# A new order of instructions on five engines of a decoder layer: the first group's scores behind the feed-forward tiles

## The reference

```
x = layernorm(x + attention(x))          # 16 heads of 32, LoRA added to the q, k, v, o projections
x = layernorm(x + x * scan(ctx * ctx))   # r = decay * r + ctx*ctx along the sequence
h = gelu(silu(bitlinear(x, w1)))         # 2048 wide; bitlinear: rms norm, round to 8 bits,
h = layernorm(h, ln_g, ln_b)             # weights rounded to -1, 0, 1
x = layernorm(x + bitlinear(h, w2))
```

## Time and profile before

| | |
|---|---|
| median of 3 runs | 1128.77 us (1127.43 to 1133.42) |
| profiled execution | 1124.67 us, its span 1122.9 us |
| busy, share of the span | PE 85%, DVE 79%, ACT 74%, POOL 54% |
| one batch (from `y(j,0)` to `y(j+1,0)`) | 60.9 us |
| mean granted clock of TensorE | 0.945 of full |

### The profile page before, as it was taken

How to read it: one execution, slowest core, us unless ns; L and a number is a source line. 1 busy time by engine, 2 the same in 40 slices (tenths; PEclk the granted TensorE clock), 3 DMA queues, 4 the chain that set the end, 5 groups by cost and what they waited for, 6 DMA issues and landing times.

```text
span 1122.9 us, 23509 instructions
## 1 busy us (share of the span) xinstructions
PE 952.4 (85%) x9388; PEld 653.1 (58%) x9388; DVE 887.3 (79%) x1470; ACT 828.3 (74%) x955; POOL 601.0 (54%) x769
## 2 busy tenths in 40 slices
PE   4878878998989898999999898989899998873424
PEld 2666656675757666665757575766667575531201
DVE  5378858888897979798988989797979898885442
ACT  3456677887879787878788787978787878775651
POOL 3213428384756657482938475565738293747250
PEclk8989898999999999999999999999999999977756
DMA  8512100213131212213221313122221222121112
GB/s 309 208 71 101 43 27 20 69 49 78 49 78 20 75 52 51 62 53 69 48 79 49 78 48 78 20 70 57 50 58 57 69 48 60 49 59 28 40 28 66
DMA packets 106350, 73.67 MB, mean 66 GB/s; under 512 B 91385, under 2 KB 91385, under 8 KB 104450
## 3 DMA queue, kind: packets, MB, share of 16 engines
q1 hardware_dynamic: 105522, 70.34, 23.4%
q10 hardware_dynamic: 720, 1.84, 0.5%
HBM read 41.73 MB, written 8.40 MB: 45 GB/s over the span
## 4 chain that ended last, share of the span: by engine, by line
PE 49%; DVE 31%; ACT 7%; issue 6%; DMA 4%; POOL 2%; SPq 1%; POOLq 0%; ACTq 0%; DVEq 0%
PE bank L1081 17%; PE bank L1202 10%; PE bank L1195 9%; DVE neg_max L793 3%; PE wave L1128 3%; DVE fz L912 3%; DVE h L907 3%; DVE stats L842 3%; PE bank L1140 2%; PE wave L1104 2%; DMA xqT<-xq 2%; PE bank L1144 2%; PE bank L1196 2%; DVE xq L898 2%; DVE rows L858 2%
## 5 line engine op out<-in xcount | busy, mean ns | idle before, releaser
L793 DVE TENSOR_REDUCE neg_max<-wave 128x8 f32<-128x2048 f32 x64 | 146.2, 2285 | 56.8 <-PE wave L1104 56.8
L1195 PE MATMUL bank<-w,xqT 128*128 128x512 fp8e4 x512 | 133.9, 385 | 44.9 <-DMA xqT<-xq 36.9
L479 POOL TENSOR_TENSOR h<-h,g_tile 128x2048 f32<-128x2048 f32 x32 | 148.4, 4638 | 40.4 <-ACT h L642 40.4
L1202 PE MATMUL bank<-w,hqT 128*128 128x512 fp8e4 x512 | 124.7, 400 | 43.3 <-DMA hqT<-h 43.3
L559 ACT ACTIVATE probs<-wave 128x1024 f32<-128x1024 f32 x128 | 124.0, 1021 | 30.9 <-PE wave L1128 30.8
L621 ACT ACTIVATE h<-bank,qx 128x512 f32<-128x512 f32 x128 | 87.0, 687 | 44.6 <-PE bank L1196 44.3
L597 ACT ACTIVATE rows<-rows,rstd 128x512 f32<-128x512 f32 x96 | 74.4, 807 | 55.7 <-POOL rstd L394 19.7
L1202 PEld LDWEIGHTS bank<-w,hqT 128*128 128x128 bf16 x512 | 49.7, 102 | 112.2 <-issue 62.0
L1195 PEld LDWEIGHTS bank<-w,xqT 128*128 128x128 bf16 x512 | 48.5, 99 | 110.6 <-issue 47.1
L378 POOL TENSOR_SCALAR attn_hi<-attn 128x256 fp32r<-128x256 f32 x64 | 26.2, 409 | 157.5 <-DVE attn L826 148.7
L907 DVE TENSOR_TENSOR h<-h,b_tile 128x2048 f32<-128x2048 f32 x32 | 75.5, 2359 | 36.5 <-POOL h L479 36.5
(11 more groups left out here) (151 smaller groups left out, 2821.3 us busy)
## 6 DMA issues: line engine op xcount, KB each, us to landing
ctx_sb<-ctxT SPq DMA_DIRECT2D x16, 512.0 KB, 3.7
rows<-x SPq DMA_DIRECT2D x16, 512.0 KB, 4.0
out<-rows SPq DMA_DIRECT2D x32, 256.0 KB, 2.0
xT_in<-xT SPq DMA_DIRECT2D x15, 512.0 KB, 4.7
h<-w1T SPq DMA_DIRECT2D x4, 1024.0 KB, 5.4
h<-w2T SPq DMA_DIRECT2D x4, 1024.0 KB, 5.6
h<-Wq SPq DMA_DIRECT2D x1, 1024.0 KB, 5.8
h<-Wk SPq DMA_DIRECT2D x1, 1024.0 KB, 9.6
```

The lines of the kernel that those rows point to most:

```text
L479: po.tensor_tensor(h_of(b, q)[:, :], h_of(b, q)[:, :], g_tile[:, :], ALU.mult).then_inc(S["g_mul"], 1)
L793: dv.tensor_reduce(neg_max[:, :, :], wave[:, :, :].rearrange("p j (t k) -> p j t k", t=NT), axis=AX_X, op=ALU.max, negate=True).then_inc(S ...
L1195: pe.matmul(p[:, :], xqT[:, q, kc, :], w1[:, kc, n * FW:(n + 1) * FW], start=(kc == 0), stop=False)
L1202: last = pe.matmul(p[:, :], hqT[:, k, :], w2[:, k, :], start=(k == 0), stop=(k == FC - 1))
```

## The change

The lists of four engines are put in another order, SyncE's list stays.

TensorE: `scores(j,0)` moves from the end of body j-1 to the start of body j, `shiftT(j,0)` between the two halves of `o(j-1,0)`, `shifted(j,0)` behind them. The eight feed-forward tiles so run without anything between them. `weighted(j,3)` stands ahead of `qk(j+1,1)`, and `v(j+1,0)` is split in two around `shiftT(j,3)`. Tiles f take banks 6, 7 and 4 in turn instead of 6 and 7. Since bank 4 is that of `weighted`, f2 waits for `attn_norm(j,3)`, and `weighted(j,0)` for the SiLU of the seventh tile (index 6).

VectorE: `maxima(j,0)` opens the body; `z_max(j-2,0)` stands behind `layernorm2_sum`, `qk_lo(j+1,0)` ahead of `attn_norm(j,2)`, `z_add(j-2,1)` behind `quantise_z(j-2,0)`, `scan(j)` ahead of `qk_lo(j+1,1)` and `quantise_z(j-2,1)`.

ScalarE: `z_square` of both halves stands behind `normalise(2)`, the second one as late as behind `zq_store(j-2,0)`; `probs_of(j,3)` comes ahead of `xq_store(j-1)`, and that ahead of `v_store(j+1,1)`, `normalise(3,j-3,1)` and `ctx_square(j)`; `qk_hi(j+1,1)` stands between the two `silu`.

GpSimd: `inverse_std2` and `x_rms` come ahead of `g_mul(j-2,1)`, and `attn_split(j,3)` ahead of `z_rms(j-2,1)` and `res2(j-1)`.

```diff
@@ -205,6 +205,7 @@
                  ("v", 1, -1, "v_stored", 2)]
         users += [("f", u, 1, "silu_done", u + 1) for u in range(8)]
         bank_no = {u[:2]: 6 + i % 2 for i, u in enumerate(users)}
+        bank_no.update({("f", u): (6, 7, 4)[u % 3] for u in range(8)})
         def bank_of(name, index):
             return bank[bank_no[name, index]]
@@ -520,23 +521,21 @@
                     x_lo(j + 1)
                 if alive(j, 0):
                     attn_split(j, 1)
-                if alive(j, 2):
-                    g_mul(j - 2, 1)
+                if alive(j, 1):
+                    inverse_std2(j - 1)
+                    x_rms(j - 1)
                 if alive(j, 3):
                     inverse_std3(j - 3, 1)
-                if alive(j, 1):
-                    inverse_std2(j - 1)
-                    x_rms(j - 1)
-                if alive(j, 2):
+                if alive(j, 2):
+                    g_mul(j - 2, 1)
                     z_rms(j - 2, 0)
                 if alive(j, 0):
                     attn_split(j, 2)
+                    attn_split(j, 3)
+                if alive(j, 2):
+                    z_rms(j - 2, 1)
                 if alive(j, 1):
                     res2(j - 1)
-                if alive(j, 2):
-                    z_rms(j - 2, 1)
-                if alive(j, 0):
-                    attn_split(j, 3)
             batches(body)
@@ -684,6 +683,8 @@
             v_store(0, 0)
             def body(j):
+                if alive(j, 0) and j > 0:
+                    shiftT(j, 0)
                 if alive(j, 0):
                     probs_of(j, 0)
                 if j == 0:
@@ -725,32 +726,31 @@
                     probs_of(j, 2)
                 if alive(j, -1):
                     qk_hi(j + 1, 0)
-                if alive(j, 2):
-                    z_square(j - 2, 0)
-                    z_square(j - 2, 1)
                 if alive(j, 1):
                     normalise(2, j - 1, 0)
                     normalise(2, j - 1, 1)
+                if alive(j, 2):
+                    z_square(j - 2, 0)
+                if alive(j, 0):
+                    shiftT(j, 3)
                 if alive(j, -1):
                     v_store(j + 1, 0)
                 if j < 2:
                     ternary_store(4 * j + 0)
                     ternary_store(4 * j + 1)
                 if alive(j, 0):
-                    shiftT(j, 3)
-                    ctx_square(j)
+                    probs_of(j, 3)
+                if alive(j, 1):
+                    xq_store(j - 1)
                 if alive(j, -1):
                     v_store(j + 1, 1)
                 if alive(j, 3):
                     normalise(3, j - 3, 1)
-                if alive(j, 1):
-                    xq_store(j - 1)
-                if alive(j, 0):
-                    probs_of(j, 3)
-                if alive(j, -1):
-                    qk_hi(j + 1, 1)
+                if alive(j, 0):
+                    ctx_square(j)
                 if alive(j, 2):
                     zq_store(j - 2, 0)
+                    z_square(j - 2, 1)
                 if j < 2:
                     ternary_store(4 * j + 2)
                     ternary_store(4 * j + 3)
@@ -759,7 +759,7 @@
                 if alive(j, 1):
                     silu(j - 1, 0)
                 if alive(j, -1):
-                    shiftT(j + 1, 0)
+                    qk_hi(j + 1, 1)
                 if alive(j, 1):
                     silu(j - 1, 1)
                     gelu(j - 1, 0)
@@ -996,6 +996,8 @@
             dv.tensor_copy(b1_p[2], b1_r2).then_inc(u_b1, 1)
             def body(j):
+                if alive(j, 0) and j > 0:
+                    maxima(j, 0)
                 if alive(j, 3):
                     layernorm3_sum(j - 3, 0)
                 if alive(j, 1):
@@ -1017,39 +1019,38 @@
                     qk_lo(j, 3)
                 if alive(j, 3):
                     layernorm3_sum(j - 3, 1)
-                if alive(j, 2):
-                    z_max(j - 2, 0)
                 if alive(j, 1):
                     layernorm2_sum(j - 1, 0)
                     layernorm2_sum(j - 1, 1)
                 if alive(j, 2):
-                    z_add(j - 2, 1)
+                    z_max(j - 2, 0)
                 if j < 2:
                     ternary(4 * j)
                     ternary(4 * j + 1)
                 if alive(j, 0):
                     maxima(j, 3)
-                    attn_norm(j, 2)
                 if alive(j, -1):
                     qk_lo(j + 1, 0)
+                if alive(j, 0):
+                    attn_norm(j, 2)
                 if alive(j, 1):
                     quantise_x(j - 1)
                 if alive(j, 2):
                     quantise_z(j - 2, 0)
+                    z_add(j - 2, 1)
                 if j < 2:
                     ternary(4 * j + 2)
                     ternary(4 * j + 3)
-                if alive(j, -1):
-                    maxima(j + 1, 0)
                 if alive(j, 0):
                     attn_norm(j, 3)
+                if alive(j, 2):
+                    z_max(j - 2, 1)
+                if alive(j, 0):
+                    scan(j)
                 if alive(j, -1):
                     qk_lo(j + 1, 1)
                 if alive(j, 2):
-                    z_max(j - 2, 1)
                     quantise_z(j - 2, 1)
-                if alive(j, 0):
-                    scan(j)
             batches(body)
@@ -1133,6 +1134,8 @@
                 wait(pe, "attn_done", b, c)
                 wait(pe, "v_stored", b, 2)
+                if c == 0 and b >= 2:
+                    wait(pe, "silu_done", b - 2, 6)
                 wait(pe, "probs_ready", b, 2 * (c + 1))
                 for kt in range(NT):
                     for i in range(GH):
@@ -1162,11 +1165,21 @@
                 wait(pe, needs, b, k)
                 return bank[where]
+            def v_terms(q, kcs):
+
+                return [(xT_hi[:, kc, q * P:(q + 1) * P], xT_lo[:, kc, q * P:(q + 1) * P],
+                         w_hi["v"][:, kc, :], w_lo["v"][:, kc, :]) for kc in kcs]
+
+            def v_first_half(j, q):
+                p = take(j, "v", q, "x_lo", j + 1, 1)
+                split_product(p[:, :], v_terms(q, (0, 1)), final=False)
+
+            def v_second_half(j, q):
+                split_product(bank_of("v", q)[:, :], v_terms(q, (2, 3)), first=False).then_inc(S["v_ready"], 1)
+
             def v(j, q):
-                p = take(j, "v", q, "x_lo", j + 1, 1)
-                split_product(p[:, :], [(xT_hi[:, kc, q * P:(q + 1) * P], xT_lo[:, kc, q * P:(q + 1) * P],
-                                         w_hi["v"][:, kc, :], w_lo["v"][:, kc, :])
-                                        for kc in range(KC)]).then_inc(S["v_ready"], 1)
+                v_first_half(j, q)
+                v_second_half(j, q)
             def o_terms(q, kcs):
@@ -1190,6 +1203,8 @@
             def f(j, u):
                 q, n = divmod(u, NF)
+                if u == 2 and alive(j, 0):
+                    wait(pe, "attn_done", j, 4)
                 p = take(j, "f", u, "xqT_loaded", j - 1, 16)
                 for kc in range(KC):
                     pe.matmul(p[:, :], xqT[:, q, kc, :], w1[:, kc, n * FW:(n + 1) * FW], start=(kc == 0), stop=False)
@@ -1234,13 +1249,20 @@
             pe.wait_ge(u_bo, 1)
             def body(j):
+                if alive(j, 0) and j > 0:
+                    scores(j, 0)
                 if alive(j, 3):
                     y(j, 0)
                 if j == 1:
                     pe.wait_ge(u_lo_late, 2)
                 if alive(j, 1):
                     o_first_half(j, 0)
+                if alive(j, 0) and j > 0:
+                    shiftT(j, 0)
+                if alive(j, 1):
                     o_second_half(j, 0)
+                if alive(j, 0) and j > 0:
+                    shifted(j, 0)
                 if alive(j, 0):
                     qk(j, 2)
                     scores(j, 1)
@@ -1275,32 +1297,25 @@
                     scores(j, 3)
                     weighted(j, 2)
                 if alive(j, -1):
-                    v(j, 0)
+                    v_first_half(j, 0)
                 if alive(j, 0):
                     shiftT(j, 3)
                 if alive(j, -1):
-                    v(j, 1)
-
+                    v_second_half(j, 0)
                 if alive(j, 0):
                     shifted(j, 3)
                 if alive(j, -1):
+                    v(j, 1)
+                if alive(j, 0):
+                    weighted(j, 3)
+                if alive(j, -1):
                     qk(j + 1, 1)
-                    scores(j + 1, 0)
-                if alive(j, 0):
-                    weighted(j, 3)
                 if j == 1:
                     pe.wait_ge(u_tern, 8)
                     pe.wait_ge(u_b1_in, 16 * NPART)
                 if alive(j, 1):
-                    for u in range(NF):
+                    for u in range(2 * NF):
                         f(j, u)
```

(19 more changed lines are left out.)

## The result

The changed kernel takes 1141.99 us (median of 4 runs, 1140.75 to 1142.93) against 1128.83 for the kernel before beside it: a ratio of 1.0125 [1.0096, 1.0154]. Its profiled execution took 1140.75, with a span of 1138.8 us against 1122.9. It is slower by 1.25%, as forecast and inside the range, but by 13 us where 30 were forecast.

What follows compares the result with a forecast made beforehand. TensorE was taken as the bound, its own work some 57 of 61 us a period. 13 x 0.5 = +6.5, 13 x 2.0 = +26 and end -2.6 made +30 us: 1154.6 profiled, 1159 as median; range 1091 to 1174.

Steps and rivals of the forecast that it cites:

- The held instruction: VectorE's L884 in quantise_x: held beside GpSimd's g_mul until that ends at 499.8, taking 1.7 us.
- If they take strict turns: VectorE's small instructions alternate with GpSimd's: x_round ends 3.35 us behind g_mul, at 503.2; 3.0 taken, so 502.8.
- The queues behind it: SyncE's store waits for normalise(3) ahead of xq's transpose: issued x_round + 2.8, f0 3.88 later at 509.5, tiles end 518.2.
- VectorE is nearly the bound and gives no cost yet: VectorE's next maximum, after quantise_z, is done 1 us before its transpose on TensorE, so no cost.
- Period at full clock: TensorE from one qk(j,2) to the next: tiles end 518.2 plus 8.55 gives 526.8 against 526.3, +0.5 us.
- 13 x 2.0 = +26: TensorE's clock falls after a 4.1 us wait before f0, costing 2.0 us in each of 13 periods, +26 us.
- The last batch: In the last batch zq_store(0) follows quantise_z(0) directly, so it and everything after come 2.6 us earlier.
- First batches: At the start, batches 0 and 1, waits for weights set the time: change 0, within 3 us.
- A: Faster rival: L884 isn't held, f0 starts at 506.5, the clock holds, -2.5 us a period: 1094 us; chance 0.25.
- B: No-change rival: the wait before f0 is there but TensorE's clock holds, +4 us: 1133 us; chance 0.13.
- C: Worse rival: g_mul gets in before L803 of the last maximum, +30 us more: 1189 us; chance 0.08.
- main case: Head start lost to GpSimd, one long TensorE wait, slow products behind it: 1159 us, 1142 to 1174; chance 0.54.

Runs made afterwards that it cites:

- e1: Changed kernel with GpSimd's g_mul(j-2,1) put back ahead of inverse_std2: 1112.27 us, 0.9863 of the kernel before.
- e3: Changed kernel with ScalarE's normalise(3,j-3,1) put ahead of xq_store(j-1): 1138.86 us, 1.01 of the kernel before.
- e7: Changed kernel with res2 in the next body and normalise(3) ahead of xq_store: 1129.04 us, 1.0006 of the kernel before.
- e2: Changed kernel with GpSimd's res2 one body later, behind inverse_std3(j-3,0): 1139.72 us, 1.0111 of the kernel before.
- e5: Kernel before, with only group 0's scores, maxima, shift copy and shifted moved behind the feed-forward tiles: 1152.46 us, 1.021 of the kernel before.
- e10: Changed kernel with tiles in banks 6 and 7 alone, without the two waits for bank 4: 1147.1 us, 1.0156 of the kernel before.
- e9: Changed kernel with g_mul ahead of inverse_std2, res2 in the next body and normalise(3) ahead of xq_store: 1099.02 us, 0.9733 of the kernel before.
- e4: Changed kernel with g_mul(j-2,1) ahead of inverse_std2 and res2 in the next body: 1110.88 us, 0.9854 of the kernel before.
- e12: Changed kernel with the three edits of e9, but group 0 in its old place and tiles in banks 6 and 7: 1104.94 us, 0.9799.

## Why the prediction was right in sign and too large

**The held instruction: right.** L884 until the end of g_mul, 1.56 us for 1.7, in every full period; the 4.43 us in the last batch were not foreseen. Taking g_mul away from it gives 30 us (e1). The Trainium skill (SBUF — State Buffer, SBUF: two separate sides) has this as its rule, whoever is first holds the shared ports for the whole instruction, and this row agrees: 1.56 us, until g_mul ends.

**"If they take strict turns", x_round at 502.8: wrong, by 1.5 us.** One instruction was held and then GpSimd gave way; x_round came at 501.3, the low bound's 501.5. "I take 3.0", chosen as nearest to the turns, rested on L893 and L898, which had been held by something that this order had moved away (res2). Even so L893 was not free: 0.69 us for 0.22, beside attn_lo. That rule of the Trainium skill, applied to every small instruction in turn, gives 503.2, and the measurement is against that use of it.

**The queues behind it: right.** Store ahead of transpose, transpose at x_round + 2.86 (2.8). From there to f0 it was 3.58 us, not 3.88. f3 waits for the SiLU behind z_square, which I had as equal to the banks' rhythm and which costs 0.6. Tiles end at 517.3 for 518.2.

**"VectorE is nearly the bound and gives no cost yet": wrong.** I had the maximum 1 us ahead of its transpose; it was 0.92 behind. The cost of the scan beside GpSimd was not in the sum: I had read where res2 went from, and not beside what it came to stand. 5.51 + 1.58 for 4.54 + 0.69 is 1.86 us, and this is the whole miss. e3 against e7, which differ by res2 alone, shows that this loop sets 61.6; e2 that taking it away uncovers TensorE's path at 61.3.

**Period at full clock, +0.5: +0.7, by errors that cancel.** Tiles end 0.9 early, the part up to qk(j,2) is 9.8 us instead of 8.55 with its new wait.

**"13 x 2.0 = +26" for the clock: the step that made the size wrong.** It was the largest term of the sum, and it measured nothing. Three things failed in it. The wait was 2.05 and not 4.1 (1.5 from x_round, 0.3 from the landing, 0.2 from TensorE's readiness). With such a wait the clock fell in four periods, not all. And where it fell it cost nothing, since VectorE was as late. The price itself depends on the slack, the time that TensorE would have waited behind f0 anyway: nothing in the changed kernel, 0.9 a period in e2, 1.4 to 1.9 in e5, 1.9 in the one of e10. My 2.0 came from the last bodies, where the products wait 9 and 14 us for their data and no other engine's lateness can take the loss in.

**The last batch, -2.6: +0.6.** Timeline after, the end of batch 15 on GpSimd and y(14,1) and y(15,0) of TensorE:

```profile
1101.23 0.19 POOL L422 TENSOR_SCALAR rstd<-mean_var 128x1 f32<-128x1 f32 x1 [5.36 <-DVE mean_var L844]
...
1102.38 4.50 POOL L480 TENSOR_TENSOR h<-h,g_tile 128x2048 f32<-128x2048 f32 x1
...
1094.52 4.89 PE L1217 MATMUL bank<-w,hqT 128*128 128x512 fp8e4 x16 [14.27 <-DMA hqT<-h]
1116.89 5.64 PE L1217 MATMUL bank<-w,hqT 128*128 128x512 fp8e4 x16 [17.48 <-DMA hqT<-h]
```

g_mul(15,1) now stands in the queue behind inverse_std3(14,1), which waits for y(14,1) at 1094.52. From it to y(15,0) it is 22.4 us, 21.8 before (1078.70 to 1100.49) and 19.4 in e1. I had followed ScalarE and VectorE through the drain, and not the queue of GpSimd. That queue also holds L884 of the last batch for 4.43 us (e1 above), in the stretch of the last two f0, which is 2.8 us longer than before.

**First batches, 0 within 3: +3.8.** It is there from the f0 of j = 2 (+4.2). Which of the edits makes it stays open: the f0 at 270.31 comes at 267.34, 266.51 and 266.47 in e3, e7 and e9, and at 267.29 in e2, but at 270.32 in e4, which has e2's edit too.

**The rivals.** A needed a free L884; it was held in every period. e1 is what A would have been, 1112, and its 1094 was too good: the period is 60.1 and not 58.3. VectorE's scan is not the main reason, since e4 without its excess is only 1.4 us better; it took e3's edit as well to come to 1099 (e9). B (the wait is there, the clock holds, 1133) came nearest as a mechanism: from 517 to 995 us that is what happened, with 0.2 us a period more than it had and the start and the end wrong. C did not occur: the maximum started at 491.9, g_mul at 495.0.

**Luck.** The low end of the main case, 1142, is what was measured, but not by its reasons. It was x_round at 501.5 with -0.8 us a period for it, +2.0 for the clock and -2.6 at the end. The x_round was right; the period got +0.7 with VectorE's late maximum in it and nothing from the clock, and start and end added 7 us that were not forecast.

## What to carry to other kernels

When an instruction moves on VectorE or GpSimd, list what it comes to stand beside on the other one, long and short: here a product of two elements stood 1.56 us behind GpSimd's multiplication, 4.43 us in the last batch, and the scan with its clip lost 1.9 us to additions. Two paths within a microsecond of each other hide each other's price; two edits that give hardly anything alone (2 and 3 us) may give 13 together, so try the pair. Price a fall of the clock only on an engine that has no other wait behind it to lose. And work that fills a wait should be moved only once the wait is gone: the move of the first group cost 24 us in the old order (e5), and with its third bank it gained 6 once f0 hardly waited (e9 against e12).

## What the runs showed of the hardware

- A VectorE product of two elements (0.17 us alone) was held for 1.56 us until a 4.65 us GpSimd product ended. In the last batch the same product was held for 4.43 us. The three small ones behind it were not held (0.17, 0.17 and 0.16), and GpSimd's power took 0.82 for 0.55; a fourth, behind x_round, was held again by attn_lo (0.69 for 0.22). Strict turns, one instruction each, did not occur.
- The scan of 128x256 takes 0.67 us alone (e2) and 1.44 as a mean beside GpSimd's additions; the two-scalar clip of 128x1024 takes 0.69 alone and 1.58; the addition of 128x512 on GpSimd takes 1.27 to 1.29 in e2, where the scan is not beside it, and about 1.65 beside it. Both engines lose; whether they share or alternate these runs do not show.
- The clock behind the same wait of TensorE (2.06 and 2.08 us, same place, same kernel) went to its lower level for 3.4 us in one period and not in the other. What decides between them was not found.
- What a fall costs the kernel depends on the waits behind it: nothing in the changed kernel, 0.9 us a period in e2, 1.4 to 1.9 in e5.
